# Two graph layers on one core: the stacked q and k operands go through a DRAM scratch in 9 transfers instead of 24 SBUF-to-SBUF ones, and the five engines' step lists are written anew

## The reference, cut to what matters

```python
# x (64, 128, 384), adj (64, 128, 128), float32; hidden 384, 12 heads of 32
h = relu(layernorm(x))
q, k, v = h @ Wq.T, h @ Wk.T, h @ Wv.T + bv             # 12 heads
scores = einsum(q, k) * 384**-0.5 + (adj + adj)          # per head
x = x + softmax(scores) @ v @ Wo.T + bo                  # attention layer
h = relu(layernorm(x))
for l in range(2):                                       # graph layer, two sublayers
    u_left, u_right = h @ (h @ W_left[l].T).T, h @ (h @ W_right[l].T).T    # / sqrt(384)
    u = where(upper triangle with diagonal, u_left, u_right), masked by adj
    e = exp(u) * adj;  att = e / sum(e)
    h = relu(layer_norm(att @ (h @ W_lin[l].T + b_lin[l])) * ln_a[l] + ln_b[l])
x = x + h
```

## Time and profile before

| | |
|---|---|
| median of 3 runs | 1622.85 us (1622.07, 1622.85, 1628.5) |
| profiled execution, its own time | 1625.41 us |
| its span, first to last instruction | 1623.7 us, mean granted TensorE clock 0.98 |
| PE busy | 1550.8 us (96% of the span) |
| DVE / ACT / POOL busy | 1146.9 / 922.7 / 457.1 us |
| q and k transfers | 768 issues on SP, 48 KB each |

### The profile page before, as it was taken

One profiled execution on the slowest core, in us unless ns is written; L12 is line 12 of the kernel. 1 busy time (PEld: TensorE's weight loads), 2 busy tenths in 40 slices (PEclk: granted clock), 3 DMA queues, 4 the chain that ended last, 5 costly groups with the idle time before them and its releaser, 6 DMA issues.

```text
span 1623.7 us, 39352 instructions
## 1 busy us (share of the span) xinstructions
PE 1550.8 (96%) x13888; PEld 1524.4 (94%) x13888; DVE 1146.9 (71%) x4303; ACT 922.7 (57%) x2155; POOL 457.1 (28%) x928
## 2 busy tenths in 40 slices
PE   3699999999999999999999999999999999999984
PEld 3699999999999999999999999999999999999974
DVE  5567777777777677776767777767777776777643
ACT  4456655566665566665556656555666655665632
POOL 4113222333232223322233323222332323332222
PEclk8789999999999999999999999999999999999996
DMA  6101112211112211112221111221111222111100
GB/s 212 40 21 41 43 50 54 53 44 31 47 44 50 54 50 30 42 44 50 53 54 43 33 45 44 50 53 50 33 40 42 53 50 53 46 30 46 31 11 20
DMA packets 116769, 76.19 MB, mean 47 GB/s; under 512 B 14282, under 2 KB 116432, under 8 KB 116576
## 3 DMA queue, kind: packets, MB, share of 16 engines
q1 hardware_dynamic: 116128, 73.06, 17.6%
q0 software_dynamic: 448, 0.60, 0.1%
HBM read 23.28 MB, written 12.58 MB: 22 GB/s over the span
## 4 chain that ended last, share of the span: by engine, by line
PE 87%; SPq 7%; DVE 2%; issue 1%; ACT 1%; DMA 1%; POOL 1%; DVEq 0%; ACTq 0%; POOLq 0%
PE bank L341 70%; SPq L297 6%; PE bank L417 5%; PE bank L347 4%; PE bank L410 3%; PE bank L401 3%; PE bank L423 1%; DMA k<-qk 1%; PE bank L435 0%; ACT prob L506 0%; DVE qk L599 0%; ACT qk L482 0%; SPq L304 0%; DMA x_sb<-x 0%; DVE weights L575 0%
## 5 line engine op out<-in xcount | busy, mean ns | idle before, releaser
L341 PE MATMUL bank<-h,weights 128*128 128x256 f32 x3456 | 429.9, 282 | 5.8 <-DVE h L740 5.1
L341 PEld LDWEIGHTS bank<-h,weights 128*128 128x128 f32 x3456 | 412.0, 190 | 6.7 <-issue 5.7
L506 ACT ACTIVATE prob<-prob,rmin 128x128 f32<-128x128 f32 x768 | 237.2, 404 | 49.9 <-DVE rmin L657 49.9
L341 PE MATMUL bank<-weights,h 128*128 128x384 f32 x1152 | 223.5, 338 | 0.0
L341 PE MATMUL bank<-hA,weights 128*128 128x256 f32 x1728 | 218.5, 283 | 1.4 <-DVE hA L599 1.4
L599 DVE TENSOR_TENSOR n<-bank,n 128x512 fp32r<-128x512 f32 x192 | 129.4, 687 | 122.8 <-ACT n L482 122.7
L341 PEld LDWEIGHTS bank<-hA,weights 128*128 128x128 f32 x1728 | 211.7, 190 | 1.7 <-DVE hA L599 1.7
L341 PEld LDWEIGHTS bank<-weights,h 128*128 128x128 f32 x1152 | 194.1, 188 | 0.0
L482 ACT ACTIVATE n<-bank 128x512 fp32r<-128x512 f32 x192 | 111.9, 606 | 113.9 <-PE bank L341 113.9
L657 DVE CUSTOM_DVE_ANT_0 prob<-bank,adj_sb 128x128 f32<-128x128 f32 x768 | 175.0, 287 | 0.2 <-issue 0.2
L482 ACT ACTIVATE qk<-bank 128x512 f16<-128x512 f32 x96 | 57.2, 595 | 170.5 <-PE bank L341 170.5
(11 more groups left out here) (107 smaller groups left out, 2652.2 us busy)
## 6 DMA issues: line engine op xcount, KB each, us to landing
q<-qk SPq DMA_DIRECT2D x384, 48.0 KB, 1.9
k<-qk SPq DMA_DIRECT2D x384, 48.0 KB, 2.0
x_sb<-x SPq DMA_DIRECT2D x32, 384.0 KB, 3.5
out<-x SPq DMA_DIRECT2D x32, 384.0 KB, 2.5
adj_sb<-adj SPq DMA_DIRECT2D x32, 128.0 KB, 2.1
prob<-w SPq DMA_DIRECT2D x4, 576.0 KB, 6.3
x<-w SPq DMA_DIRECT2D x3, 576.0 KB, 4.4
pT<-w SPq DMA_DIRECT2D x3, 576.0 KB, 5.4
```

The source lines that it names most:

```text
L341: mm = pe.matmul(out, lhsT, rhs, start=(n == 0), stop=(n == len(pairs) - 1))
L506: e = act.activation(prob[:, j, h, :], prob[:, j, h, :], ACT.Exp, bias=rmin[:, j, h:h + 1], scale=-1.0)
```

## The change

The q and k parts go from `qk` to a DRAM tensor `qk_dram` by three stores (`qs0`, `qs1`, `qs2`, one behind each QK step, 128 partitions, 256 KB each, in rows of 1 KB), and from there by three loads into `q3` and three into `k3` (192 KB each, in rows of 1.5 KB). The loads wait for the stores to have landed. The waits that `xn1` had on the stacked copies are now on the stores. The heads lie in another order in `q3` and `k3`, and the score matmuls index them so. The step lists of all engines and the banks are new.

```diff
+        qk_dram = nc.dram_tensor("qk_parts", [2, P, 2, 2 * C, T], F16).ap()
...
-        STACKED = 16 * 3 * HC
+        STACKED = 16 * 3
...
-            def stack(dst, s, first, parts):
-                for a in range(HC):
-                    for r, part in enumerate(parts):
-                        sp.dma_start(dst[D * r:D * r + D, a:NH:HC, :], qk[D * a:D * a + D, part, first:first + C, :]).then_inc(s, 16)
+            def stack(dst, s, which, parts, p):
+                for r, part in enumerate(parts):
+                    heads = qk_dram[p, :, part, which * C:which * C + C, :].rearrange("(a d) c t -> d a (c t)", d=D)
+                    sp.dma_start(dst[D * r:D * r + D, :, :].rearrange("d (a c) t -> d a (c t)", a=HC), heads).then_inc(s, 16)
...
+                elif step[:2] == "qs":
+                    k = int(step[2])
+                    ge(sp, s_q3, STACKED * (g - 1))
+                    ge(sp, s_k3, STACKED * (g - 1))
+                    wait_drained(sp, f"QK{k}", g)
+                    sp.dma_start(qk_dram[p, :, :, 2 * k:2 * k + 2, :], qk[:, :, 2 * k:2 * k + 2, :]).then_inc(s_qs[k], 16)
                 elif step in ("q3", "k3"):
...
-                    wait_drained(sp, "QK1", g)
+                    sp.wait_ge(s_qs[1], 16 * (g + 1))
                     if step == "q3":
-                        wait_drained(sp, "QK0", g)
-                        stack(q3, s_q3, 0, (HI, LO, HI))
+                        sp.wait_ge(s_qs[0], 16 * (g + 1))
+                        stack(q3, s_q3, 0, (HI, LO, HI), p)
                     else:
-                        wait_drained(sp, "QK2", g)
-                        stack(k3, s_k3, C, (HI, HI, LO))
+                        sp.wait_ge(s_qs[2], 16 * (g + 1))
+                        stack(k3, s_k3, 1, (HI, HI, LO), p)
...
-                        mm = pe.matmul(bank(step)[:, a * P:(a + 1) * P], q3[:, h, j * P:(j + 1) * P], k3[:, h, j * P:(j + 1) * P], start=True, stop=True)
+                        mm = pe.matmul(bank(step)[:, a * P:(a + 1) * P], q3[:, a * C + c, j * P:(j + 1) * P], k3[:, a * C + c, j * P:(j + 1) * P], start=True, stop=True)
...
-                    ge(act, s_q3, STACKED * g)
-                    ge(act, s_k3, STACKED * g)
+                    for k in range(3):
+                        ge(act, s_qs[k], 16 * g)
```

More of the change, by code:

```diff
@@ L71 @@
 BANK = {
[L72 to L79, removed]
+    0: ["HL10", "P02", "HL01", "HTa"],
+    1: ["T2a", "S01", "P00", "PV0", "T1a", "QK0", "WO1"],
+    2: ["N10", "U1", "S12", "C10", "S10", "AT", "P10", "PV1", "QK2"],
+    3: ["N11", "N02", "OT0", "C00"],
+    4: ["S00", "N01", "P12", "C01", "HTb", "V0"],
+    5: ["N12", "S02", "S11", "P01", "U0", "T1b", "OT1"],
+    6: ["HL11", "P11", "QK1"],
+    7: ["T2b", "N00", "C11", "HL00", "WO0", "V1"],
 }
@@ L83 @@
     "SP": [
-        ("out", -2), ("q3", 1), ("ld_x", 2), ("k3", 1), ("ld_adj", 2)],
[1 row of a table added]
     "PE": [
[5 rows of a table removed]
-    "ACT": [
[6 rows of a table removed]
-    "DVE": [
[8 rows of a table removed]
[5 rows of a table added]
+    "ACT": [
[5 rows of a table added]
+        ("HTb", 0), ("HTa", 0), ("V1", 2)],
+    "DVE": [
[7 rows of a table added]
+        ("QK1", 2), ("QK2", 2), ("WO1", 1), ("HTb.h", 0), ("HTb.l", 0), ("HTa.h", 0), ("HTa.l", 0)],
     "POOL": [
-        ("gn0", -1), ("xbo1", 1), ("xbo0", 1), ("ln2", 0), ("ml", 0), ("ln1", 2), ("gn1", -1), ("za0", -1), ("za1", -1),
-        ("mu", 0), ("zb0", -1), ("zb1", -1)],
+        ("ln2", 0), ("ln1", 2), ("ml", 0), ("gn1", -1), ("mu", 0), ("za0", -1), ("za1", -1), ("zb0", -1), ("zb1", -1),
+        ("gn0", 0), ("xbo1", 2), ("xbo0", 2)],
 }
@@ L214, in build @@
         s_q3, s_k3 = sem("q3_in"), sem("k3_in")
+        s_qs = [sem(f"qk_out{k}") for k in range(3)]
         s_exp = [[sem(f"exps{j}{c}") for c in range(C)] for j in range(G)]
@@ L239, in build @@
         SPLIT_AFTER = {
-            "ACT": {"": (0,), "xn1_1": (1,), "T1b": (2, 3), "QK0": (4, 5), "QK1": (6,), "V1": (7,), "QK2": (8,), "V0": (9,)},
-            "DVE": {"ln1_ag": (0,), "T1b": (1, 2), "QK0": (3, 4), "QK1": (5,), "QK2": (6, 7), "V1": (8,), "V0": (9,)}}
+            "ACT": {"": (0,), "xn1_1": (1,), "T1a": (2, 3), "QK0": (4, 5), "QK1": (6,), "QK2": (7,), "V1": (8,), "V0": (9,)},
+            "DVE": {"ln1_ag": (0,), "T1a": (1, 2), "QK0": (3, 4), "QK1": (5,), "QK2": (6, 7), "V0": (8,), "V1": (9,)}}
         def staged(m):
@@ L399, in run @@
                     for a in range(HC):
-                        h = c * HC + a
-                        mm = pe.matmul(bank(step)[:, a * P:(a + 1) * P], q3[:, h, j * P:(j + 1) * P], k3[:, h, j * P:(j + 1) * P], start=True, stop=True)
+                        mm = pe.matmul(bank(step)[:, a * P:(a + 1) * P], q3[:, a * C + c, j * P:(j + 1) * P], k3[:, a * C + c, j * P:(j + 1) * P], start=True, stop=True)
                     mm.then_inc(full(step), 1)
```

## The result

The change makes the kernel 0.68% faster: 1613.87 us (median of 5 runs, 1613.54 to 1615.15) against 1625.75 us before (median of 5 runs on the same chip, 1622.07 to 1628.5). The ratio is 0.9932, 95% interval 0.9913 to 0.995. The forecast was 1603, its range ended at 1613. The profiled execution has a span of 1611.7 us; before it was 1623.7, so 12.0 us went, where the sum had 20.0.

What follows compares the result with a forecast made beforehand. PE's work of 47.73 us a group was taken as the bound, with 0.16 us stall and idle times in head and tail. Head 16.5, loop 4.2, tail -0.7 sum to 20.0 us off 1622.85: 1603, range 1597 to 1613.

Steps and rivals of the forecast that it cites:

- head, first pass: First scores of the head: reach DVE at about 34.5 against 41.58 us, 7.1 us earlier (5.5 to 9).
- head, second pass: Second scores of the head: start at 75.2 against 83.68 us, 8.5 us earlier.
- behind the second scores: Head, N00 and P10 behind the second scores: a net gain of 0.9 us.
- loop: 30 repeated groups: the stall of 4.9 us goes, 0.7 us of new stall comes, 4.2 us gained (-4 to +5).
- tail: Last group to the end: later zb1 and y1 before C00, HTb.l and y0's order; 0.7 us lost (-1 to +2).
- the price of the transfer: q and k by DRAM: store 2.5 us, load 2.5 (2.0 to 3.5); drained QK2 to k landed 6.5 us (5.5 to 8).
- The other bound: Head, first pass: DVE's splits, V and statistics start at 24.4 us and, with about 2 us waiting, are done at 34.
- the transfer isn't in time in the head: Rival: DRAM completions in the head cost more than 2.5 us; 4 us, giving 1607, or 8 us, giving 1611; chance 0.13.
- the tightest margin: Loop, bank 2, S10 right behind C10: 0.14 us left, a stall of 0 to 0.3 us a group.
- the slower rival: Rival: in the loop y1 waits for zb1 on DVE and T1's drain is late for QK0; up to 1654 us; chance 0.08.
- One smaller step: Head, N00's 18 matmuls behind the second scores: most of 1.8 us back, from about 3.9 us at half clock against 2.1.

Runs made afterwards that it cites:

- The half rows: The changed kernel with each load moving half of every row (96 KB a load) from group 1 on; measured once, 1608.99 us.
- the loads from SBUF: The changed kernel with its stores, but the six loads read SBUF instead of DRAM, same 32 partitions and rows; measured once, 1613.99 us.
- the mended tail: The changed kernel with OT1 ahead of WO0 on DVE, z1_0 ahead of AT on ACT, za0 ahead of mu on POOL; 1612.75 us, ratio 0.9922.
- the transfers alone: The kernel before with the new stores and loads, all lists but SP's and the banks as before; 1614.58 us, ratio 0.9931.

## Why the prediction was right in direction and wrong in size

Its steps against what came, in us off the span:

| term | foretold | came |
|---|---|---|
| head, first pass | 7.1 | 3.1 (scores on DVE 41.58 to 38.47) |
| head, second pass | 8.5 | 6.7 (83.68 to 73.86 is 9.8, less 3.1), of it 1.5 from the clock |
| behind the second scores | 0.9 | 0.5 (10.3 less 9.8) |
| loop | 4.2 | 4.05 |
| tail | -0.7 | -2.35 |
| sum | 20.0 | 12.0 |

**The step that failed** is the price of the transfer, "a load 2.0 to 3.5, I take 2.5". The last load of k took 4.93 and 5.59 us in the head, and its median is 5.5. The bounds came from rows in which one transfer, or a row of copies issued 0.64 us apart, was in flight. Six loads of 192 KB and x are issued in under 4 us, and then the bytes count: 1.83 MB at 210 GB/s. From ld_x to the scores the prediction had 75.2 - 68.85 = 6.35 us, it took 8.84, 2.5 us more. The half rows gave 2.2 us back in this pass.

The second pass would have come out worse but for luck. From the second T1 to WO1 PE took 9.95 us where it took 11.41 before, since the granted clock was 1.00 and not 0.83. The prediction had no term for these 1.5 us, and the kernels above show that they come and go with the same steps.

In the first pass the chain is longer. The last store was foretold to have landed at 28.6; the one that q3 waits for landed at 30.35 (24.17 and 6.18 on the chain), with weights and x in the queue at 380 GB/s. Then q's three issues, which were thought done by then, came first, since q3 too waits for a landed store (1.4 us), and k's last load landed at 37.58, where 32.4 to 33.4 was foretold. The other bound moved as well. DVE's rows, beside the earlier trace rows:

```profile
25.20 0.69 DVE L607 TENSOR_TENSOR qk<-bank,qk 128x512 f16<-128x512 f32 x1 [0.41 <-ACT qk L490]
...
32.00 1.02 DVE L620 BATCH_NORM_STATS2 stats_ln<-x_sb 128x6 f32<-128x384 f32 x2 [2.10 <-DMA x_sb<-x]
...
38.47 0.06 DVE L600 MEMSET carrier<- 128x1 f32 x1 [1.99 <-PE bank L409]
```

QK2 is drained at 25.2, as foretold (24.4 to 25.0). But x came at 32.0, not at 29 to 30, so DVE was through at 36.5 and not at 34. Against the prediction's 34.5 us the scores reach DVE 4.0 us late: DVE alone would make it 2.5, and k's landing makes it 4.0. Both waited for the one queue.

**The rival** "the transfer isn't in time in the head" is the one that happened, and more of it than its 1607: it too had taken loads at 3.5 us. The Trainium skill (DMA: Bandwidth & Descriptors, section "Anatomy of one DMA") gives about 2.0 us and bytes over 436 GB/s per transfer, for GpSimd's queue. For one store of 256 KB that is an estimated 2.6 us, and the median here is 2.5. For one load of 192 KB it is an estimated 2.45, and 5.5 us were measured for k (3.0 with half the bytes), with the other loads and x in the queue. The same section's warning on writes to HBM isn't seen in the median; the one slow store on the chain (6.18 us) had the weights in the queue beside it. Nor was it the other leg's DRAM side, as the loads from SBUF showed.

**What was right.** The loop: 47.758 us a group against 47.73 and 0.02 foretold. The wait at bank 2 is there, where the prediction had the tightest margin (waits of after, 100 to 1530 us: in total, times, longest):

```profile
PEld bank L409 <- ACT c_sb L551: 5.3, 30, 0.4
```

Once a group, 0.18 us on the average, of which little reaches the period: it is 0.03 longer than with the old lists. y1's wait for zb1 didn't break the loop, so the slower rival didn't happen. T2a stood 1.82 us idle and not 4.31, since QK2's drain no longer holds up ln2. The early drain itself is worth 7.3 us of the new lists' head. One smaller step failed behind the second scores: of the 1.8 us that N00 was to give back for the most part, 0.1 came.

**The tail** was mis-sized by 1.65 us. Up to C00 it lost 0.9 us (from AT to C00 50.86 us, less 2.2, against 47.80). That is the size foretold, but by luck in part: the stated reason (mu ahead of za and AT ahead of z1) fell with the mended tail, y1 in y0's place does it by the rows, and there is a wait that the prediction had not looked for, WO0's for the store `out`. Behind C00 it lost 1.5 us (41.15 against 39.66), from matmuls at the lower clock, and that had no term.

The best version takes the transfers and QK2's early drain into the old lists, with the three stores ahead of everything that waits for a landing: ratio 0.9912 against 0.9932. The intervals overlap, so that it beats the change isn't shown.

## What to carry to other kernels

When a change makes issues cheaper, the limit moves on to the bytes: price a burst of transfers by what it moves over the rate of the queue, and not by the landing of one transfer that had the queue to itself. In a list that one engine takes in order, all stores belong ahead of the first step that waits for one of them to land. Undo a compound change by halves: here the transfers alone gave the whole gain, and the new order added nothing to them. And before two heads or tails are compared from one trace each, look at the granted clock of stretches with the same steps: here it moved them by up to 1.8 us.

## What the runs showed of the hardware that was not expected

- Loads of 192 KB into 32 partitions, together with x and a store, came at 210 GB/s with the DMA engines busy 0.88 of the time; into 96 partitions, in rows of 2 KB, at 230 GB/s (share 0.81). Weights, x and stores on 128 partitions moved 380 GB/s. How much of this is partitions and how much is rows wasn't separated.
- The same PE steps from the second T1 to WO1 took 9.7 to 9.95 us in eight kernels (granted clock 1.00) and 11.1 to 11.5 in six (0.83 to 0.85), and two kernels with the same steps there fell on either side.
- Three issues on SP took 1.3 us for loads from DRAM into 32 partitions, and 2.0 to 2.55 us for the same loads read from SBUF.
- The 18 matmuls of N00 behind the second scores took between 3.2 and 4.2 us in all kernels (3.24 behind a gap of 0.16 us, 3.48 behind 2.21 and 4.13 behind 2.26, 4.07 behind 1.66, 3.20 behind 1.84, 4.10 behind 2.37, 3.93 behind 3.45), with no order by the last gap, and 2.3 us in a busy stretch.
